# A kernel of attention, experts, selective scan and trees on one core: the turning of attention's probabilities moves to the head of a step, and a pair of scores waits once for its two banks

## The reference

```python
NUM_HEADS, NUM_GROUPS, HEADS_PER_GROUP, KEY_WIDTH = 16, 4, 4, 64
# L0_attn(X, Wq, Wk, Wv, Wpost), X: (8, 512, 256)
Q = (X @ Wq).reshape(n, s, NUM_GROUPS, HEADS_PER_GROUP, KEY_WIDTH)
K = (X @ Wk).reshape(n, s, NUM_GROUPS, KEY_WIDTH)
V = (X @ Wv).reshape(n, s, NUM_GROUPS, VALUE_WIDTH)
raw = jnp.einsum('bsgwe,btge->bstgw', Q, K * scale)
attn = jax.nn.softmax(raw, axis=2)
A = jnp.einsum('bstgw,btge->bsgwe', attn, V).reshape(n, s, NUM_HEADS * VALUE_WIDTH)
s = X + A @ Wpost
...
xn = _layernorm(x)
x = x + L0_attn(xn) * silu(L0_ffn(xn))
xn = _layernorm(x)
x = x + L1_attn(xn) * silu(L1_ffn(xn))
```

## Time and profile before

| | us |
|---|---|
| median of 3 runs | 2903.2 (2891.9 to 2904.88) |
| profiled execution, own time | 2905.59 |
| its span | 2903.8 |
| TensorE busy in the span | 2455.9 |
| VectorE, ScalarE, GpSimd busy | 1956.8, 1815.7, 1736.8 |
| mean granted clock of TensorE | 0.926 of full |

### The profile page before, as it was taken

How to read it: one execution, slowest core, us unless ns; L and a number is a source line. 1 busy time by engine, 2 the same in 40 slices (tenths; PEclk the granted TensorE clock), 3 DMA queues, 4 the chain that set the end, 5 groups by cost and what they waited for, 6 DMA issues and landing times.

```text
span 2903.8 us, 37611 instructions
## 1 busy us (share of the span) xinstructions
PE 2455.9 (85%) x12740; PEld 1377.3 (47%) x12744; DVE 1956.8 (67%) x2958; ACT 1815.7 (63%) x3324; POOL 1736.8 (60%) x1416
## 2 busy tenths in 40 slices
PE   6786889998789989898989898989898889977771
PEld 4444567765344454445444454445444544453331
DVE  5778755533266766676667676766676677779898
ACT  3556834445377776766666766785677577756753
POOL 1000165407656886877587668776876697645566
PEclk9888999999898999999999898999998999988895
DMA  4000278855545575555564465447543654466766
GB/s 151 24 14 5 68 196 249 238 150 98 92 98 102 115 154 126 112 105 122 127 116 92 93 155 105 89 91 169 106 88 74 160 113 89 88 143 150 172 160 148
DMA packets 282049, 344.44 MB, mean 119 GB/s; under 512 B 66176, under 2 KB 211535, under 8 KB 281857
## 3 DMA queue, kind: packets, MB, share of 16 engines
q0 software_dynamic: 84080, 175.67, 32.8%
q1 hardware_dynamic: 175264, 144.80, 17.2%
q10 hardware_dynamic: 22512, 21.57, 2.2%
HBM read 198.23 MB, written 26.80 MB: 77 GB/s over the span
## 4 chain that ended last, share of the span: by engine, by line
PE 34%; ACT 14%; issue 10%; POOL 8%; DVE 8%; DMA 0%; POOLq 0%; DVEq 0%; ACTq 0%
PE bank L1795 5%; PE bank L1784 5%; PE bank L1931 5%; PE bank L1960 4%; PE bank L1746 3%; POOL arena L1671 3%; DVE bank L1546 3%; PE bank L1853 2%; ACT PT L1035 2%; POOL acc_sb L1649 2%; ACT bank L1154 2%; ACT Pr L1015 2%; PE bank L1807 2%; PE bank L2028 1%; POOL arena L1677 1%
## 5 line engine op out<-in xcount | busy, mean ns | idle before, releaser
L1671 POOL TENSOR_TENSOR arena<-arena 128x512 f32<-128x512 f32 x512 | 860.7, 1758 | 32.4 <-DVE arena L1537 32.4
L1649 POOL DMA_INDIRECT acc_sb<-ybuf,slot_idx x256 | 421.8, 1648 | 148.3 <-DMA ybuf<-arena 64.3
L1246 DVE TENSOR_REDUCE negmax<-bank 128x1 f32<-128x512 f32 x512 | 341.6, 678 | 246.8 <-PE bank L1784 246.4
L1677 POOL TENSOR_TENSOR arena<-arena 128x512 f32<-128x512 f32 x192 | 282.5, 1471 | 359.3 <-DVE arena L1546 359.1
L1154 ACT ACTIVATE bank<-arena,A_sb 128x512 f32<-128x512 f32 x512 | 354.9, 696 | 194.3 <-DVE arena L1551 170.4
L1784 PE MATMUL bank<-Kp,Qp 64*128 64x512 f32 x1024 | 416.2, 686 | 66.8 <-ACT Pr L1015 51.3
L1546 DVE TENSOR_TENSOR_SCAN bank<-bank,arena 128x512 f32<-128x512 f32 x320 | 390.9, 1221 | 86.3 <-ACT bank L1154 77.7
L1015 ACT ACTIVATE Pr<-bank,negmax 128x512 f32<-128x512 f32 x512 | 352.9, 689 | 144.9 <-DVE negmax L1246 142.7
L1795 PE MATMUL bank<-ident,Pr 128*128 128x128 f32 x2048 | 349.0, 295 | 108.5 <-ACT PT L1035 60.3
L1035 ACT COPY PT<-bank 128x512 f32<-128x512 f32 x512 | 300.1, 586 | 192.8 <-PE bank L1795 187.5
L1795 PEld LDWEIGHTS bank<-ident,Pr 128*128 128x128 f32 x2048 | 225.7, 146 | 285.2 <-issue 100.2
(11 more groups left out here) (218 smaller groups left out, 3897.5 us busy)
## 6 DMA issues: line engine op xcount, KB each, us to landing
arena<-arena POOLq DMA_DIRECT2D x255, 512.0 KB, 5.0
arena<-bc_dram SPq DMA_DIRECT2D x256, 256.0 KB, 3.8
ybuf<-arena ACTq DMA_DIRECT2D x64, 256.0 KB, 4.1
arena<-in_w_gate SPq DMA_DIRECT2D x64, 128.0 KB, 2.9
arena<-in_w_up SPq DMA_DIRECT2D x64, 128.0 KB, 4.0
arena<-in_w_down SPq DMA_DIRECT2D x64, 128.0 KB, 4.8
arena<-in_X SPq DMA_DIRECT2D x8, 512.0 KB, 8.7
s_sb<-in_X SPq DMA_DIRECT2D x8, 512.0 KB, 6.1
```

What stands on the lines that cost most here:

```text
L1246: dve.tensor_reduce(negmax[:, m % RING_STAT:m % RING_STAT + 1], bank[m % RING_S_ATT][:, :], AX.X, ALU.max, negate=True).then_inc(att_max, 1)
L1649: pool.indirect_dma_start(acc_sb[:, i, :], None, ybuf, bass.IndirectOffsetOnAxis(ap=slot_idx[:, b * TILES + i, k:k + 1], axis=0), bounds_c ...
L1671: pool.tensor_tensor(st_sb[:, g % RING_S, :], u_sb[:, size_slot(b, cb), :], B_sb[:, load % RING_BC, :], ALU.mult).then_inc(ssm_input, 1)
L1677: pool.tensor_tensor(v, v, C_sb[:, load % RING_BC, :], ALU.mult).then_inc(ssm_c_pool, 1)
```

## The change

The turning of TensorE's step and the copy of ScalarE's step go from the end of a step to its head, and LAG_T goes from 2 to 3. Step n now begins with the turning and the copy of place n-3, which before ended step n-1. Ahead of a pair of scores, TensorE now waits for Exp of place n-2, which frees the second score's bank; before, only the second score waited for it. The counts in the other waits (products on bank 3, spread, turning) are adapted to the new order and mean the same instructions.

```diff
-LAG_EXP, LAG_T, LAG_AV, LAG_RAN = 1, 2, 4, 5
+LAG_EXP, LAG_T, LAG_AV, LAG_RAN = 1, 3, 4, 5
...
@@ class Scalar @@
             def att_step(self, b, n):
+                m = n - LAG_T
+                if 0 <= m < ATT_STEPS:
+                    place = b * ATT_STEPS + m
+                    w.wait_ge(att_turned, place + 1)
+                    w.wait_ge(att_av, (place - RING_P) // 2 + 1 if m >= RING_P else b * ATT_STEPS // 2)
+                    act.copy(PT[:, m % RING_P, :, :].rearrange("p a b -> p (a b)"), bank[PROBT][:, :]).then_inc(att_pt, 1)
                 m = n - LAG_EXP
...
                     self.copy_k(b, (p + 1) // 2, PROJ)
-                m = n - LAG_T
-                if 0 <= m < ATT_STEPS:
-                    place = b * ATT_STEPS + m
-                    w.wait_ge(att_turned, place + 1)
-                    w.wait_ge(att_av, (place - RING_P) // 2 + 1 if m >= RING_P else b * ATT_STEPS // 2)
-                    act.copy(PT[:, m % RING_P, :, :].rearrange("p a b -> p (a b)"), bank[PROBT][:, :]).then_inc(att_pt, 1)
...
@@ class Tensor @@
             def score(self, b, n):
+
+                if n + 1 >= RING_S_ATT:
+                    w.wait_ge(att_exp, b * ATT_STEPS + n + 1 - RING_S_ATT + 1)
                 for m in (n, n + 1):
...
             def att_step(self, b, n):
 
+
                 p, at = n // PAIR_STEPS, n % PAIR_STEPS
+                if 0 <= n - LAG_T < ATT_STEPS:
+                    self.turn_p(b, n - LAG_T)
                 if n % 2 == 0:
...
                     self.values(b, n - 1 - LAG_AV, (2, 3) if self.has_other(p, at - 1) else (0, 1, 2, 3))
-                if 0 <= n - LAG_T < ATT_STEPS:
-                    self.turn_p(b, n - LAG_T)
```

More of the change, by code:

```diff
@@ L1751, in product_k @@
                 w.wait_ge(att_invbc, PAIRS * b + 2 * g - 1)
-                w.wait_ge(att_pt, b * ATT_STEPS + PAIR_STEPS * (2 * g - 1) + 6 - LAG_T)
+                w.wait_ge(att_pt, b * ATT_STEPS + PAIR_STEPS * (2 * g - 1) + 7 - LAG_T)
                 self.product(Wk_sb[:, :, g * P:(g + 1) * P], PROJ).then_inc(att_kmm, 1)
@@ L1757, in product_q @@
                 w.wait_ge(att_invbc, PAIRS * b + p - 1)
-                w.wait_ge(att_pt, b * ATT_STEPS + PAIR_STEPS * (p - 1) + 4 - LAG_T)
+                w.wait_ge(att_pt, b * ATT_STEPS + PAIR_STEPS * (p - 1) + 5 - LAG_T)
                 self.product(Wq_sb[:, :, p * P:(p + 1) * P], PROJ).then_inc(att_qmm, 1)
@@ L1790, in turn_p @@
                 w.wait_ge(att_v, 2 * (b + 1))
-                w.wait_ge(att_q, PAIRS * b + min(p + 1 + (at >= 4), PAIRS))
-                w.wait_ge(att_k, GROUPS * b + min(p + (at >= 6), PAIRS - 1) // 2 + 1)
-                w.wait_ge(att_invbc, PAIRS * b + (p - (at < 2) if p else 0))
+                w.wait_ge(att_q, PAIRS * b + min(p + 1 + (at > 4), PAIRS))
+                w.wait_ge(att_k, GROUPS * b + min(p + (at > 6), PAIRS - 1) // 2 + 1)
+                w.wait_ge(att_invbc, PAIRS * b + (p - (at <= 2) if p else 0))
                 for c in range(TILES):
@@ L1815, in spread @@
                 w.wait_ge(att_k, GROUPS * b + min(p + 1, PAIRS - 1) // 2 + 1)
-                w.wait_ge(att_pt, b * ATT_STEPS + PAIR_STEPS * (p + 1) + 2 - LAG_T)
+                w.wait_ge(att_pt, b * ATT_STEPS + min(PAIR_STEPS * (p + 1) + 3 - LAG_T, ATT_STEPS))
                 for i in range(TILES):
```

## The result

| | before | after |
|---|---|---|
| median of the runs, us | 2901.7 (4 runs, 2891.9 to 2904.9) | 2852.1 (4 runs, 2846.1 to 2853.1) |
| span of the profiled execution, us | 2903.8 | 2844.3 |
| attention of batches 2 to 7 (first to last Exp), us | 184, 179, 189, 178, 190, 192 | 169, 168, 177, 174, 184, 183 |
| mean granted clock | 0.926 | 0.932 |

The ratio is 0.9832, with an interval from 0.9815 to 0.9849: 49.6 us faster by the medians. The sign is right, the size is wrong by more than a factor of two, and the time came out near the rival "more than the sum" (2846).

What follows compares the result with a forecast made beforehand. Attention's loop through TensorE and ScalarE was taken to bound the recurrence stretches. Terms -42 + 17 + 0 = -25 us, five sixths of it -21, gave a forecast of 2883 us, range 2848 to 2916.

Steps and rivals of the forecast that it cites:

- more than the sum: Rival: all 85 us of the scores' lateness go and VectorE and GpSimd wait less; -60 us, 2846 us; chance 0.12.
- What bounds the kernel: In six recurrence stretches, attention's loop through TensorE and ScalarE sets the pace; 85 us of TensorE's busy time are half-done pairs.
- The mechanism: A decay between copy and Exp moves ahead of the copy, where ScalarE stood; Exp and pair end 0.63 us earlier.
- The gain, -42: 77 late pairs in the six stretches, least of three limits at each: 42 us saved, bounds 0 and 85.
- The cost of the later copies, 17: Odd steps' copies behind decays make turnings late at 42 places: 17 us together, bounds 0 and 69.
- Five sixths: In one of six stretches the chain runs over GpSimd and issue, so -25 us was cut to -21 us.
- The pair's wait, 0: First score now also waits for the second's bank: cost taken as 0, bounds 0 and 56 us.
- The rest of the program: Routing, tables, experts, trees and the last 300 us: change taken as nothing.
- Another chain: Rival: the recurrence's chain over GpSimd sets the pace in all stretches; saving some 5 us, 2900 us; chance 0.21.
- The copies: Rival: nothing to spare at later copies, so they cost 69 us instead of 17; 2932 us; chance 0.07.
- The clock: Rival: waits leave TensorE empty and its clock falls at 13 places, 36 us in all; 2921 us; chance 0.10.
- The signs: Expected: copies' waits under 149 us, scores' line near 200, L1154 under 2%, turnings' waits up 17, stretches 3 to 5 shorter.

Runs made afterwards that it cites:

- e13_changed: The changed kernel measured again without any edit, on another chip: 2847.6 us, 0.9827 of the kernel before.
- e1_split: The changed kernel without the wait for two banks, so only the second score of a pair waits, as before: 2873.0 us, 0.9848 of the kernel before.
- e2_pair: The kernel before with only the wait of a pair of scores moved ahead of the first score: 2909.8 us, 0.9986 of the kernel before.
- e3_copy: The kernel before with only ScalarE's copy moved to the head of the next step, TensorE's order unchanged: 2894.2 us, 0.9916 of the kernel before.
- e7_hybrid: The changed kernel with both turnings and copies of a pair in the odd step, moving only the even-to-odd border: 2872.9 us, 0.9851 of the kernel before.
- e11_late_odd: The changed kernel, but in batches 2 to 7 both turnings and copies of a pair in the odd step: 2843.8 us, 0.9806 of the kernel before.

## Why the prediction was right, and where it was wrong

**What bounds the kernel: right.** The 85 us of pairs that stood half done were there to be had (85.0 in the 975 us as well); 78.7 us of busy time went. The Trainium skill, "Perfetto Trace Analysis", section "Identifying the Most-Contended Engine", warns against reading headroom from TensorE's occupancy, and this case agrees: 12740 instructions, 106 us less busy.

**The mechanism: right**, at the place of the earlier trace rows to 0.03 us, and by the runs on the two borders.

**The gain, -42: wrong, this is the step that failed.** I took for each place the least of three: the lateness, the inserted work, and the time that ScalarE stood ahead of the copy. The third is no limit. Where ScalarE did not stand, the inserted work still leaves the way of the Exp; it delays the copy instead, and that is paid, if at all, at whatever waits for bank 3 next. The cap counted this payment as a gain not made, and always at its full size. Place by place, over 76 of the places in the six stretches: at 14 ScalarE stood under 0.1 us, the cap allows 0.1 us in all, and the pairs there were busy 33.4 us before and 17.7 after (with 6.7 us of idle time ahead of them). At 61 it stood over 0.6 us each, but the work between was often longer; the cap allows 42.6 us, and the pairs went from 120.4 to 69.8. Without the cap, by the lesser of lateness and inserted work, these places give 76 us. Measured were 78.7 in the scores' busy time and, by adding up the idle times of the same stretches, another 7 in their waits (18.2 to 11.3), 86 in all.

**The cost of the later copies, 17: too small by 2.6 times**, and for a reason that can be named. The count had turnings only. Turnings waited 27 us more in the six stretches (20.0 to 47.2, the same adding up). But bank 3 has other users: the spread waited 25 us and the products 12 where neither had a wait, since they now stand right behind a turning of their own step; and the turning behind the spread waited 19 less. Together 27 + 25 + 12 - 19 = 45 us. What these waits were behind fits: of the 84 us that TensorE waited for copies there, 24 (39 times) were for a copy that ScalarE did directly behind a decay, without standing, and 36 (44 times) directly behind an activation of the next batch's input side (L1095 to L1132). The prediction moved the turning ahead of the other work on bank 3 without asking what that work then waits for.

**The sum.** In the six stretches: -79 - 7 + 45 = -41, measured -41.1. That it comes out is bookkeeping rather than proof, since busy and idle time of one engine always add up to the stretch (-75.0 and +33.9). The forecast's terms gave -25 there. The gain was 44 us larger and the cost 28 us larger, and the two errors partly cancelled, by luck.

**Five sixths: wrong.** The stretch with the chain over GpSimd got shorter too, from 157.38 to 148.57 (its whole attention 179 to 168). Its chain still ends over GpSimd, so the chain's engine was no evidence that attention has no say there. A reason that fits, but was not tested apart: GpSimd was busy 120.77 of 157.38 us and is busy 123.18 of 148.57, so it had slack, and what it waits for are scans, which wait for decays, which come earlier (its wait of 343 us for scans is 296 after).

**What the account leaves over.** The attentions as wholes, first to last Exp, went from 1111 to 1054 us. So beside the 41 us, some 15 lie in the first four and the last three steps of the six attentions (135.5 to 120.1 us by the starts of Exp). The prediction's stretches took in most of these steps and its sum had them at the same rate as all others; why they gain more, no run took apart. A part is chance of where they fall: in e13_changed, the same kernel, they take 125.0.

**The pair's wait, 0: right** (e1_split, e2_pair). **The rest of the program: right.** Of the 59.5 us between the spans, 57 lie in these six attentions; the first 300 us gave 4 and the experts took 4. (The profiled execution of after is its fastest; the medians are 49.6 us apart.)

**The rivals.** "More than the sum" named the right things, all the lateness and the relief of VectorE, and its 2846 is 6 us off; 0.12 was too little for it, since the cap was all that spoke against it. That it came so close is luck in part: it had the cost at 17 instead of 45, and nothing for the 15 us at the ends of the attentions. "Another chain" fell with the stretch over GpSimd. "The copies" had the right direction, a cost well over 17, and the wrong gain beside it.

**The clock** did not slow the kernel: 0.932 after 0.926, and in e2_pair, with 109 us of plain standing ahead of the scores instead of 32, it is 0.926 as before. It went the other way: in the six stretches TensorE was at the lower level for 44.4 us after, 78.0 before, and busy there for 40.5 instead of 70.5. By the estimate used with e2_pair this is worth at most some 12 of the 41 us. The forecast had no such term. No run holds the clock fixed, so how much of it is a gain beside the order's, and how much only follows from it, stays open; e3_copy against e2_pair shows 43.8 us without it. The Trainium skill, "TensorE: Matmul & The Clock Gate", section "Why this matters for your kernels", asks for no long idle gaps between bursts of matmuls. The 101 gaps of e2_pair are 1.1 us on average and 7.7 at most, and no run here shows a price of them.

**The signs.** Right: the copies' wait (149 to 93), the scores' line (196), the smaller and moved wait for Exp, nothing outside. Wrong: L1154 did not leave the chain (4.1% and 5.8%), because it went from ahead of one link to ahead of another; the waits for copies rose by 66 us rather than 17 (29 + 25 + 12); the attentions lost 4 to 15 us each instead of 3 to 5. And one sign was worthless: e2_pair shows a scores' line just as short with no gain.

## What to carry to other kernels

When work moves from one link of a loop to another, write down the gain and the cost as two sums over all places, the full lateness on one side and all users of the delayed buffer on the other; don't cap the first by slack that belongs to the second. If an engine overlaps two instructions, a wait between them is counted as busy for as long as the first one runs (1.12 us here; what is longer shows as idle, as in the earlier trace rows). So compare the line's busy time with its count times the time of an undisturbed one, and believe a shorter line only if idle time didn't take its place. And a hand-written order can differ by stage: here the copy wants to cross the border everywhere, the turning only where the filler runs beside the experts.

## What the runs showed of the hardware

The two scores of a pair lie on partitions 0 to 63 and 64 to 127 and run beside each other: four instructions took 1.13 us where two alone took 1.12. Holding the first back for the second has no cost that could be measured (0.9986, 0.9968 to 1.0004).

The chips were not alike in one stage. The kernel before has a median of 2915.7 us on the chip of the first experiments, and of 2899.9 and 2899.1 on two others. The difference lies in the experts' stage: attention 1, which spans it, takes 391 us in e2_pair against 373 in the kernel before, and 397 in e1_split against 377 in the changed kernel. In the recurrence's stretches the chips agree: 936.9 us in e1_split and 934.0 after, 919.9 in e7_hybrid and 922.4 in e11_late_odd. 16 us is a third of what was measured here, so a ratio between chips would have misled; what in that stage differs, no run took apart.
